# A graph kernel of four gather passes: tiles gathered once into a ring that is read by register addresses

## The reference

```
xj = xl[src]
e = leaky_relu(xj + xr[dst], 0.2)
logits = e @ att
alpha = exp(logits - segment_max(logits)[dst]) / segment_sum(...)[dst]
out = segment_sum(alpha[:, None] * xj, dst)
```

## Time and profile before

| | |
|---|---|
| time, median of 3 runs | 14942.71 us (14898.92 to 14956.18) |
| profiled execution, span from first to last instruction | 12937.2 us |
| profiled execution, time beside its span | not recorded; the median is 2005.5 us above the span |
| PE busy | 10759.5 us, 83% of the span |
| DVE busy | 7923.7 us, 61% |
| ACT busy | 5625.6 us, 43% |
| POOL busy | 9422.6 us, 73% |
| mean granted TensorE clock | 0.774 |

### The profile page before, as it was taken

How to read it: one execution, slowest core, us unless ns; L and a number is a source line. 1 busy time by engine, 2 the same in 40 slices (tenths; PEclk the granted TensorE clock), 3 DMA queues, 4 the chain that set the end, 5 groups by cost and what they waited for, 6 DMA issues and landing times.

```text
span 12937.2 us, 281212 instructions
## 1 busy us (share of the span) xinstructions
PE 10759.5 (83%) x62317; PEld 8677.3 (67%) x62317; DVE 7923.7 (61%) x29130; ACT 5625.6 (43%) x14105; POOL 9422.6 (73%) x8593
## 2 busy tenths in 40 slices
PE   5888887788888888888888886999999878888886
PEld 4666666666666666666666665777777656666664
DVE  7666666666666665555555555333333468888887
ACT  1555555455555553333333335344444553333334
POOL 3777777577777758888888885777777447777775
PEclk7999999899999966666666667555555689999997
DMA  3222222422222224444444445222222222222222
GB/s 96 55 55 55 55 55 55 131 66 55 55 55 55 55 43 39 39 39 39 39 39 39 39 40 130 57 56 55 55 55 55 55 67 62 62 63 62 62 63 61
DMA packets 808952, 748.00 MB, mean 58 GB/s; under 512 B 264685, under 2 KB 691174, under 8 KB 808254
## 3 DMA queue, kind: packets, MB, share of 16 engines
q0 software_dynamic: 453440, 550.05, 23.8%
q1 hardware_dynamic: 354814, 191.38, 5.6%
HBM read 548.62 MB, written 192.13 MB: 57 GB/s over the span
## 4 chain that ended last, share of the span: by engine, by line
PE 48%; issue 11%; DMA 10%; DVE 7%; POOL 3%; ACT 2%; DVEq 1%; POOLq 0%; SPq 0%; ACTq 0%
PE bank L734 12%; DMA scatter_s<-dst_side 7%; PE bank L718 6%; PE bank L721 6%; PE bank L719 5%; PE bank L1194 4%; PE bank L1200 3%; PE bank L1209 2%; DMA rows<-gather_c,edge_sb 2%; PE bank L703 2%; PE bank L743 2%; POOL rows L685 2%; POOL scatter_s L1161 1%; DVE dst_side L1287 1%; PE bank L1203 1%
## 5 line engine op out<-in xcount | busy, mean ns | idle before, releaser
L1161 POOL DMA_INDIRECT scatter_s<-dst_side x1664 | 2568.7, 1544 | 554.2 <-issue 283.5
L821 ACT ACTIVATE oh_e<-bank,weight,minus_w 128x128 f32<-128x128 f32 x4992 | 1879.1, 456 | 1439.0 <-PE bank L743 1372.4
L933 DVE SCALAR_TENSOR_TENSOR agg<-agg,rescale,bank 128x130 f32 x4992 | 1681.8, 337 | 1302.3 <-PE bank L734 1074.6
L719 PE MATMUL bank<-rows,ident 128*128 128x128 f32 x9984 | 2138.3, 300 | 0.0
L685 POOL DMA_INDIRECT rows<-gather_b,edge_sb x1664 | 1623.5, 976 | 608.9 <-issue 327.6
L685 POOL DMA_INDIRECT rows<-gather_c,edge_sb x1664 | 1678.9, 1009 | 529.1 <-issue 337.5
L685 POOL DMA_INDIRECT rows<-gather_a,edge_sb x1664 | 1622.9, 975 | 555.3 <-issue 321.7
L685 POOL DMA_INDIRECT rows<-gather_s,edge_sb x1664 | 1574.0, 946 | 571.9 <-issue 378.8
L734 PE MATMUL bank<-rows,oh_e 128*128 128x130 f32 x9984 | 1869.5, 343 | 34.3 <-DVE agg L933 17.8
L734 PEld LDWEIGHTS bank<-rows,oh_e 128*128 128x128 f32 x9984 | 1603.1, 242 | 244.3 <-issue 210.0
L857 ACT ACTIVATE lrelu<-bank 128x512 f32<-128x512 f32 x1248 | 745.6, 597 | 2336.9 <-PE bank L719 2302.7
(11 more groups left out here) (345 smaller groups left out, 18972.2 us busy)
## 6 DMA issues: line engine op xcount, KB each, us to landing
rows<-gather_a,edge_sb POOLq DMA_INDIRECT x1664
rows<-gather_b,edge_sb POOLq DMA_INDIRECT x1664
scatter_s<-dst_side POOLq DMA_INDIRECT x1664, 3.3
rows<-gather_s,edge_sb POOLq DMA_INDIRECT x1664
rows<-gather_c,edge_sb POOLq DMA_INDIRECT x1664
rows<-scatter_s SPq DMA_DIRECT2D x56, 455.0 KB, 6.2
scatter_s<-zeros SPq DMA_DIRECT2D x64, 390.0 KB
edge_sb<-edge_tab SPq DMA_DIRECT2D x520, 40.0 KB
```

Of the source, the lines that this page charges most:

```text
L719: e.matmul(o, ident[:, :], rows[:, it.slot(), g, 0:P], start=False, stop=True).then_inc(L.side.sem, 1)
L821: e.activation(oh_e[:, g % 8, :], bank[7][:, (g % CH) * P:(g % CH + 1) * P], ACT.Relu, bias=weight[:, it.slot(2, 2), g:g + 1], scale=minus ...
L933: e.scalar_tensor_tensor(old, old, rescale[:, it.slot(2, 2), g:g + 1], sum_bank(g)[:, (g % 2) * AW:(g % 2) * AW + L.aw], ALU.mult, ALU.add ...
L1161: e.indirect_dma_start(scatter_s[k], bass.IndirectOffsetOnAxis(ap=S_.target[:, it.slot(1), g:g + 1], axis=0), S_.summed[:, g % 8, :], None ...
```

## The change

The first three passes (E0, E1, E2) get a name for a signal, and with it `by_tile`. POOL then gathers TT = 1568 tiles, each once, into a ring of 64 places (the same buffer), by a table of source indices that the preparation writes (`tile_tab`). SP loads that table by groups of 16 tiles, counts up one signal for every tile that has landed (nine tiles later in its order), and lets POOL go on by four tiles when PE's block sums have freed their places; which sums these are stands in the table. PE reads from the table of a group, in two register loads of 26 values, where each step's target block and its tile's place lie, for the side products and for the block sums, and how many tiles must have landed. The tables of a group are loaded from ACT's queue. In E2 the source score comes by a second product per step, of the identity with one column of the ring, and DVE copies the sum out of PSUM; the side products alternate between two banks. In the last pass PE's 16 addresses come by two register loads of 8.

```diff
@@ build @@
+RING = U * G
+QUAD = 4
+SIGNAL_LAG = 9
...
+    NGT = -(-(S - NB + 1) // G)
+    TT = NGT * G
+    NGX = NGT + 2
+    TW = G + QUAD
...
+    tile_tab = dram("tile_tab", (NGX, P, TW), I32)
+    HG = G // 2
+    HROW = 3 * HG + NCH // 2
+    RC = G + 2 * HROW
@@ sp_prep, pe_prep, dve_prep @@
+            e.dma_start(src_i.rearrange("p (c q) -> p c q", q=P), a["src"].rearrange("(c p) q -> p c q", p=P)).then_inc(tiles_in, 16)
...
+                if c == TILES_SAVED_AT:
+                    w.wait_ge(tiles_kept.at(0))
+                    e.dma_start(tile_tab.rearrange("g p k -> p g k"), tile_stage).then_inc(tables_saved, 16)
...
+            w.wait_ge(tiles_ready.at(0))
+            for c in range(SC):
+                ins = e.transpose(bank[4 + c // 4][:, c % 4 * P:(c % 4 + 1) * P], src_f[:, c * P:(c + 1) * P], ident[:, :])
+            ins.then_inc(tiles_turned.sem, 1)
...
+            e.tensor_copy(src_f, src_i).then_inc(tiles_ready.sem, 1)
...
+            for b in range(4):
+                n = min(4 * GC, NGX - b * 4 * GC)
+                ins = e.tensor_copy(tile_stage[:, b * 4 * GC:b * 4 * GC + n, 0:G], bank[4 + b][:, 0:n * G].rearrange("p (g k) -> p g k", k=G))
@@ registers @@
+        def sides_at(e, it):
+            lo = G
+            hi = G + HROW
+            return (places(e, mybir.EngineType.PE, it, 0, lo, lo + HG, (NB - 1) * P)
+                    + places(e, mybir.EngineType.PE, it, 0, hi, hi + HG, (NB - 1) * P))
+
+        def half_at(e, it, h):
+            lo = G + h * HROW
+            if not it.runs(0, NG):
+                return None, None, places(e, mybir.EngineType.PE, it, 2, lo + HG, lo + 2 * HG, (RING - 1) * XW), None
+            v = places(e, mybir.EngineType.PE, it, 0, lo, lo + HROW, (NB - 1) * P)
+            slots = [x.with_bounds(min_val=0, max_val=(RING - 1) * XW) for x in v[HG:3 * HG]]
+            return v[0:HG], slots[0:HG], slots[HG:], [nc.s_assert_within(x, 1, TT) for x in v[3 * HG:]]
@@ SP and POOL of the three passes @@
+        def sp_tiles(e, L):
...
+            def turn(it):
+                if it.runs(SIGNAL_LAG, TT):
+                    w.wait_ge(L.rows_in.at(it, lag=SIGNAL_LAG))
+                    e.sem_inc(L.landed.sem, 1)
...
+                full = it.n >= RING
+                if it.n % G == 0:
+                    w.hold_ge(L.index_in.at(tile_group(it)))
+                    index(tile_group(it, 2))
+                    if full:
+                        _, v = nc.values_load_multi_w_load_instructions(
+                            tile_idx[0:1, tile_group(it).slot(), G:TW], engines=[mybir.EngineType.SP], min_val=0, max_val=S // CH)
+                        needs["now"] = v
+                if it.n % QUAD == 0:
+                    if full:
+                        w.hold_ge((L.block.sem, needs["now"][it.n % G // QUAD] + L.block.base))
+                    e.sem_inc(L.go.sem, 1)
                 if it.j is None:
-                    for table, z0, z1 in L.zeroing[it.n::PEEL]:
+                    for table, z0, z1 in L.zeroing[it.n:it.n + 1]:
...
+        def pool_tiles(e, L):
+            w = On(e, anchor)
+            w.wait_ge(L.opened.at(0))
+
+            def turn(it):
+                if it.n % QUAD == 0:
+                    w.hold_ge(L.go.at(tile_quad(it)))
+                slot = it.slot(0, RING)
+                e.indirect_dma_start(pool_rows[:, slot * XW:slot * XW + L.width], None, L.src_rows,
+                                     bass.IndirectOffsetOnAxis(ap=tile_idx[:, slot // G, slot % G:slot % G + 1], axis=0)
+                                     ).then_inc(L.rows_in.sem(it), 16)
+            tile_turns(e, TT, 0, turn)
@@ pe_edges: side, block_sums, turn @@
+                if L.by_tile:
+                    w.hold_ge((L.landed.sem, need[c % 2]))
+                else:
+                    w.wait_ge(L.gat[c].at(it))
                 if L.vector:
-                    w.wait_ge(L.gat[c].at(it))
                     w.wait_ge(L.larger.at(it, c - 2) if c >= 2 else L.larger.at(it, c + 2, lag=1))
                 elif c == 0:
-                    w.wait_ge(L.score.at(it, lag=1))
+                    w.wait_ge(L.score.at(it, lag=2))
...
-                        e.matmul(o, ident[:, :], rows[:, it.slot(), g, 0:P], start=False, stop=True).then_inc(L.side.sem, 1)
+                        r = pool_rows[:, bass.ds(where[f], P)] if L.by_tile else rows[:, it.slot(), g, 0:P]
+                        e.matmul(o, ident[:, :], r, start=False, stop=True).then_inc(L.side.sem, 1)
                     else:
-                        e.matmul(bank[2][:, g:g + 1], oh, dst_flat[:, bass.ds(at[g], 1)], start=True, stop=True).then_inc(L.side.sem, 1)
...
+                        o = bank[2 + it.slot(0, 2)][:, g:g + 1]
+                        e.matmul(o, oh, dst_flat[:, bass.ds(at[f], 1)], start=True, stop=False)
+                        e.matmul(o, ident[:, :], pool_rows[:, P:][:, bass.ds(where[f], 1)], start=False, stop=True).then_inc(L.side.sem, 1)
...
-                r = (xw[:, (g // CH) % 2, (g % CH) * AW:(g % CH) * AW + AW] if L.wide else rows[:, it.slot(2), g, 0:XW])
+                r = xw[:, (g // CH) % 2, (g % CH) * AW:(g % CH) * AW + AW] if L.wide else pool_rows[:, bass.ds(where[g % HG], XW)]
...
                 for c in range(NCH):
+                    if L.by_tile and c % 2 == 0 and (now or two):
+                        at, where, old, need = half_at(e, it, c // 2)
@@ act_edges, turn @@
+                if L.by_tile and it.runs(-1, NG) and (it.j is not None or it.n + 1 >= U):
+                    ahead = Turn(it.n + 1, it.j)
+                    w.hold_ge(L.edist.at(it, NCH - 1, lag=U - 1))
+                    w.hold_ge(L.acc.at(it, 0, lag=U - 1))
+                    w.hold_ge(L.tab.at(ahead, lag=U))
+                    step_tables(e, L, ahead)
@@ dve_edges, third pass @@
-                        for c in range(NCH):
-                            w.wait_ge(L.gat[c].at(it))
-                        e.tensor_tensor(logit[:, 0:G], bank[2][:, 0:G], rows[:, u, :, P:P + 1].rearrange("p g o -> p (g o)"),
-                                        ALU.add).then_inc(L.score.sem, 1)
+                        e.tensor_copy(logit[:, 0:G], bank[2 + it.slot(0, 2)][:, 0:G]).then_inc(L.score.sem, 1)
```

More of the change, by code:

```diff
@@ L172, in turns, with tile_turns, tile_group, tile_quad @@
         turn(Turn(i))
+def tile_turns(eng, n, depth, turn):
+    peel = RING + n % RING
+    for t in range(peel):
+        turn(Turn(t, None, RING))
+    with eng.Fori(0, (n - peel) // RING) as j:
+        for t in range(RING):
+            turn(Turn(peel + t, j, RING))
+    for t in range(n, n + depth):
+        turn(Turn(t, None, RING))
+def tile_group(it, ahead=0):
+    return Turn(it.n // G + ahead, it.j, RING // G)
+def tile_quad(it):
+    return Turn(it.n // QUAD, it.j, RING // QUAD)
 def build(nc, a, out):
@@ L666, in turn, with index @@
-                for hd in range(L.heads):
-                    e.dma_start(step_sb[hd * G:(hd + 1) * G, u, 0:L.SW], step_tab[bass.ds(i * G, G), 0:L.SW]).then_inc(L.tab.sem(it), 16)
+                step_tables(e, L, it)
+            turns(e, NG, 0, turn)
+        def sp_tiles(e, L):
+            w = On(e, anchor)
+            needs = {}
+            def index(it):
+                u, i = it.slot(), it.number()
+                e.dma_start(tile_idx[:, u, :], tile_tab[bass.ds(i, 1), :, :].rearrange("o p k -> (o p) k")).then_inc(L.index_in.sem(it), 16)
+            def turn(it):
+                if it.runs(SIGNAL_LAG, TT):
+                    w.wait_ge(L.rows_in.at(it, lag=SIGNAL_LAG))
+                    e.sem_inc(L.landed.sem, 1)
+                if not it.runs(0, TT):
+                    return
+                full = it.n >= RING
[10 more added lines that the diff above has]
+                    e.sem_inc(L.go.sem, 1)
@@ L668, in turn @@
                 if it.j is None:
-                    for table, z0, z1 in L.zeroing[it.n::PEEL]:
+                    for table, z0, z1 in L.zeroing[it.n:it.n + 1]:
                         e.dma_start(table[z0 * P:z1 * P, :].rearrange("(p b) f -> p (b f)", p=P), zeros[:, 0:(z1 - z0) * XW]
                                     ).then_inc(L.zeroed, 16)
-            turns(e, NG, 0, turn)
+            for i in range(U):
+                step_tables(e, L, Turn(i))
+            index(Turn(0))
+            index(Turn(1))
@@ L757, in turn @@
                     if now:
-                        side(it, c, at)
+                        side(it, c, at, where, need)
                     if L.vector and c < 2 and now:
@@ L867, in act_edges @@
                 onehot_by_node(Turn(0), 1, 0)
[L868 removed]
+            turns(e, NG, 2, turn, ahead=int(L.vector or L.by_tile))
         def dve_edges(e, L):
```

153 lines of the change are left out of this document (97 added, 56 removed).

## The result

The changed kernel takes 16375.16 us (median of 4 runs, 16364.47 to 16419.46) against 14935.04 for the kernel before (4 runs, 14898.92 to 14956.18). The ratio is 1.0973, 95% interval [1.0952, 1.0994]. The forecast was 15395 us with a range of 15220 to 15640: the sign was right, the size too small by 980 us.

A forecast was written before the change was run, and what follows sets the result against it. It took POOL's gather pace to bound the first two passes and PE the third. Terms -123 - 123 + 710 - 25 + 5 + 8 = +452 us gave span 13389 and 15395 us, range 15220 to 15640.

The forecast's parts named there:

- the one on register loads: PE's two address loads a group, 26 values each: hidden behind queued work, value 0, at most 2.5 us a group.
- The product of the third pass: Third pass, PE: 3328 added fp32 identity product records at 0.2135 us, covered by nothing, +710 us.
- rival (c): Weight loads alone limit the third pass: it grows by 222 us, total 14932 us; chance 0.05.
- Around the span: Whole program: 2005.5 us of the median time lie outside the profiled span of 12937.2 us and stay unchanged.
- The gathers: POOL, 96 fewer gathers a pass at 1.28 us: -123 us in each of the first two passes, nothing in the third.
- ACT's table loads: Four table loads a group moved from SP's queue to ACT's: value 0, at most 177 us.
- Preparation: Before the passes: transposes, a conversion, copies and a table of short rows, value 8 us, bounds 0 and 30.
- The last pass: PE's one load of 16 becomes two of 8: hidden behind POOL, 0 to 115 us.
- Rival (a): The clock rises in the third pass, PE reaches its upper level and POOL bounds it: 14540 us; chance 0.10.
- Rival (b): First two passes gain nothing, as register loads and ACT's DMA issues meet on PE's path: 15640 us; chance 0.10.
- the last sign it gave for being wrong: First pass: PE busy without pause and POOL waiting would show the forecast wrong.
- its own range: Total with the added product at 0.2135 to 0.233 us, preparation 0 to 30, half of Rival (b): 15330 to 15560 us.

The follow-up runs named there:

- the repeated run: The kernel before, run again unchanged with its span listed: 14942.56 us, span 14940.7 us.
- the aligned kernel: The changed kernel with two unused values after each half of a group's 52 addresses, so the second half starts at value 44, not 42: 15377.57 us, 1.0303.
- run 194: No separate run: the repeated run, whose first pass takes 194 us from the first side product to that of the ninth group; whole time 14942.56 us.

## Why the prediction was wrong

**The step that failed** is the one on register loads: "Value 0. Both bounds: 0, and if a longer load were wholly in the open 2 x 1.8 - 1.1 = 2.5 us a group". Both of its parts were wrong. The size was taken in proportion to the values, from one row. The runs show two lengths: from a start that is a multiple of four values, about 0.27 us for four (20 values 1.357, 16 values 1.10, 8 values 0.59; 26 values 2.10, which is six fours and two single ones), and about 0.24 us for every value from the other starts that were run, 18, 34 and 42, each two past a multiple of four (8 values 1.95, 16 values 3.80, 26 values 6.15). The second half starts at value 42: 8.25 us a group, 7.15 more than before, where 2.5 was the upper bound. And "it runs while PE works off what is queued" doesn't hold for the long load: PE's row shows 5.52 us of nothing behind it. Moving the second half by two values gave 998 of the 1440 us back, so this is shown.

A section of the Trainium skill, "Runtime: NRT & Kernel Launch", Instruction fetch mechanics, has about 200 ns for each register of such a load, from HBM; an estimate from it would have been 26 x 0.2 = 5.2 us. In this case, from SBUF, it holds about for the load that starts badly (0.24) and not for the other (0.067).

**What a load costs** is not its length. In the kernel before, one load more or longer cost 0.09 to 0.10 of their time (99 of 1120, 164 of 1580 us), both together 0.15, up to 7.6 us of loading a group; in the kernel with the ring 0.31 from 2.7 to 4.2 us a group, and 0.47 or 0.71 from 4.2 to 8.25, by the place of the slow load. So the amount of loading alone doesn't set the price: 7.6 us a group were paid at 0.15 in the one kernel, the step to 8.25 at three to five times that in the other. That PE's sequencer, which the ring gives more to do, has less in reserve there is argued and not shown.

**The product of the third pass**: 3328 x 0.2135 = 710 us of work, measured 685. "Nothing covers it" was wrong: the program grew by 128 us and the pass by 130. The step rested on 39.4 us of idle time in 800, of the unusual execution; in the repeated run the pass has 655 us. With the product a group of the third pass does take near the 27.1 us of the forecast (2813 / 104 = 27.0), but from 25.8 (2683 / 104) and not from 20.5. The 222 us of rival (c) are nearer to the 130, but its reason, weight loads alone, isn't needed: PE as a whole had the idle time.

**Around the span.** "2005.5 us lie around the span, which I leave as they are": they lie in the four passes, which every timed run had. That the span stood 13% below the three times was in the table; it should have been read as a sign that the profile was of another kind of execution, and the reserves that it shows were not those of the runs to be predicted.

**The gathers**: 1.28 us each in the first two passes, nothing in the third. By themselves they are worth that in the first pass, 138 us for 104 (1.33 each), and 1.97 each in the third. With the ring they aren't seen: the aligned kernel's first two stretches are 94 and 139 us longer, not 123 shorter. Of this difference of 217 and 262 us, loads and register addresses account for about 100 (3.1 us a group more than before, at 0.31) and 20 us (a third of the 60) in each, an estimate from the prices above. Of the rest, some 100 and 140 us, about 50 and 45 lie in the first eight of the 104 groups: from the first side product to that of the ninth group the aligned kernel takes 243 and 233 us, the repeated run 194 and 188. In the first pass PE stands still twice there, while POOL gathers on:

```profile
270.68 0.58 PE L849 MATMUL bank<-oh_rows,oh_w 5*128 5x512 bf16 x1 [19.03 <-issue]
...
318.19 0.60 PE L849 MATMUL bank<-oh_rows,oh_w 5*128 5x512 bf16 x1 [43.21 <-issue]
```

Before the second of these rows ACT stands still as long (43.49 us before its slope, put down to "remote"). What ends these waits, no row says; they and the rest stay open. A POOL that runs further ahead by itself lengthened the first pass by 75 us, and the ring lets it run further ahead; that this is the cause was not tried.

**ACT's table loads**, value 0: their place changes nothing that can be told; their whole price wasn't isolated. **Preparation**: 12 to 15 us more before the first gather, forecast 8; the zeroing wasn't isolated. **The last pass**: forecast hidden, and it is (-18 us), although one of its loads is 1.95 us.

**Rival (a)** did not come: the clock stays at 0.50 in the third pass of every kernel, at 96% busy too. The Trainium skill's "TensorE: Matmul & The Clock Gate", Why this matters for your kernels, would have a TensorE that is kept busy at full clock; the third pass disagrees again. **Rival (b)** named the right meeting, register loads on PE's path, with a third of the size. Of what the prediction listed as signs, 2007 us from first to last gather fell (2993 us): POOL now waits for places in the ring (2583 us in three passes of the aligned kernel). That is one half of the last sign it gave for being wrong; the other, a PE that is busy without pause in the first pass, did not come (2012 of 2993 us).

**Its sums.** The terms named for "its own range" give 15387 to 15605 us, not 15330 to 15560, and no term is given for the 15220. In rival (a) 22.4 us a group is 175 us more for the pass, not 233. None of this decides anything: 16375 lies far above every bound.

That 15395 us is nearly the time of the aligned kernel (15378) is chance: a product forecast 560 us too dear stands against gathers that gained nothing with the ring and sequencer work put at nothing.

## What to carry to other kernels

Before a row of addresses is cut into parts that an engine loads into registers, see that each part starts at a multiple of four values, and cost the load from a row with the same start and count; two unused values were worth 1000 us here. Compare the profile's span with the times of the runs before any idle time in it is counted as cover. What a register load costs can't be read from its length: here it was between a tenth and seven tenths of it, by the kernel, the place and what stood beside it, so a cost that was once hidden needn't stay so when more is put beside it.

## What was not expected of the hardware

A register load from SBUF took 0.27 us for every four values from a start that is a multiple of four values, and 0.24 us for each value from a start two past such a multiple. The repeated run has 6058.6 us of waits put down to "remote", in one of which the engine goes on 5.4 us after TensorE's recorded end; one execution of the same program has none and was 13% shorter; what decides between them is open. Letting gathers start four steps earlier made the kernel 4.05% slower, mostly in the eight-head pass; why is open too.
